# A projection stage without a loop, its low parts taken from PSUM, and the value bias added in attention

## The reference, cut to what matters

```python
qkv = x @ c_attn_w.T + c_attn_b
q, k, v = (heads(t) for t in jnp.split(qkv, 3, axis=2))      # 16 heads of 16
q_lat = q @ q2l_w.T + q2l_b                                  # 32 latents a head
k_lat = k @ kv2l_w.T + kv2l_b
v_lat = v @ kv2l_w.T + kv2l_b
q_lat = q_lat * cos + _rotate_half(q_lat) * sin
k_lat = k_lat * cos + _rotate_half(k_lat) * sin
q_for_k = q_lat @ wqk_w.T + wqk_b
att = jnp.einsum('bhql,bhkl->bhqk', q_for_k, k_lat) * L ** (-0.5)
y_lat = jnp.einsum('bhqk,bhkl->bhql', softmax(causal(att)), v_lat)
```

## Time and profile before

| | us |
|---|---|
| median of 3 runs (3117.6 to 3118.45) | 3118.36 |
| the profiled execution | 3112.8 |
| its span, first to last instruction | 3111.2 |
| busy PE / DVE / ACT / GpSimd | 2844.3 / 2273.6 / 1858.7 / 776.4 |
| projection, to attention's first load | 452.35 |
| attention, from there to its last y | 1794.3 |

### The profile page before, as it was taken

How to read it: one execution, slowest core, us unless ns; L and a number is a source line. 1 busy time by engine, 2 the same in 40 slices (tenths; PEclk the granted TensorE clock), 3 DMA queues, 4 the chain that set the end, 5 groups by cost and what they waited for, 6 DMA issues and landing times. The chain is left out here.

```text
span 3111.2 us, 50281 instructions
## 1 busy us (share of the span) xinstructions
PE 2844.3 (91%) x16538; PEld 1923.9 (62%) x16538; DVE 2273.6 (73%) x5659; ACT 1858.7 (60%) x3718; POOL 776.4 (25%) x701
## 2 busy tenths in 40 slices
PE   7888957999999999999999999999889997899990
PEld 5677744555555555555555555555367775799990
DVE  7999967888888888888888888888134543445443
ACT  4666632576667666666766676666535443546544
POOL 5777851010000001000110000010024444123220
PEclk9999986899999999999999999999989998899995
DMA  4666674242243234314332432340083220434316
GB/s 153 225 224 223 217 233 105 52 101 54 52 103 78 54 76 97 69 43 102 77 78 52 103 78 54 76 95 14 11 299 117 93 76 20 118 71 109 69 21 223
DMA packets 259647, 320.07 MB, mean 103 GB/s; under 512 B 70578, under 2 KB 157787, under 8 KB 258144
## 3 DMA queue, kind: packets, MB, share of 16 engines
q1 hardware_dynamic: 241760, 294.09, 33.4%
q0 software_dynamic: 17664, 23.19, 3.9%
HBM read 182.76 MB, written 143.95 MB: 105 GB/s over the span
## 5 line engine op out<-in xcount | busy, mean ns | idle before, releaser
L803 ACT ACTIVATE att_probs<-att_score_bank 128x512 f32<-128x512 f32 (+3 forms) x2560 | 1159.0, 551 | 608.5 <-PE att_score_bank L732 600.3
L840 DVE TENSOR_REDUCE att_partial_max<-att_max_bank 128x1 f32<-128x512 f32 x1536 | 1004.9, 687 | 124.3 <-PE att_max_bank L720 118.8
L720 PE MATMUL att_max_bank<-att_k_st,att_q_st 96*128 96x512 f32 (+3 forms) x2560 | 906.4, 389 | 31.8 <-DMA att_ident<-in_ident 20.9
L732 PE MATMUL att_score_bank<-att_q_st,att_k_st 98*128 98x512 f32 (+3 forms) x2560 | 924.5, 390 | 10.1 <-DMA att_q_st<-att_max_rows 7.6
L732 PEld LDWEIGHTS att_score_bank<-att_q_st,att_k_st 98*128 98x128 f32 x2560 | 481.8, 191 | 273.2 <-ACT att_probs L803 145.7
L720 PEld LDWEIGHTS att_max_bank<-att_k_st,att_q_st 96*128 96x128 f32 x2560 | 489.4, 193 | 244.7 <-DVE att_partial_max L840 100.7
L844 DVE CUSTOM_DVE_ANT_0 att_edge_sum<-att_max_bank,att_edge 128x128 f32<-128x128 f32 (+3 forms) x1024 | 482.0, 484 | 165.2 <-PE att_max_bank L720 164.7
L826 POOL TENSOR_SCALAR_AFFINE_SELECT att_probs<-att_probs 128x512 f32<-128x512 f32 x256 | 162.5, 635 | 1615.1 <-ACT att_probs L803 1615.1
L746 PE MATMUL att_acc_bank<-att_probs,att_v_st 128*32 128x512 f32 (+3 forms) x5120 | 544.2, 538 | 1.8 <-POOL att_probs L826 0.9
L210 POOL TENSOR_TENSOR proj_op_low<-proj_turned,proj_op_high 128x512 fp32r<-128x512 f32 x192 | 275.0, 1462 | 59.1 <-ACT proj_op_high L332 58.9
L746 PEld LDWEIGHTS att_acc_bank<-att_probs,att_v_st 128*32 128x32 f32 x5120 | 131.9, 109 | 245.2 <-issue 140.3
(11 more groups left out here) (221 smaller groups left out, 3887.3 us busy)
## 6 DMA issues: line engine op xcount, KB each, us to landing
qk_parts<-proj_parts SPq DMA_DIRECT2D x64, 1024.0 KB, 4.6
att_q_st<-qk_parts SPq DMA_DIRECT2D x192, 256.0 KB, 4.0
att_k_st<-qk_parts SPq DMA_DIRECT2D x192, 256.0 KB, 6.1
v_tokens<-proj_v_tok SPq DMA_DIRECT2D x64, 256.0 KB, 4.4
att_v_st<-v_tokens SPq DMA_DIRECT2D x64, 256.0 KB, 6.9
exp_w<-in_ew SPq DMA_DIRECT2D x16, 1024.0 KB, 8.9
dispatched<-mix_empty_rows SPq DMA_DIRECT2D x8, 1036.0 KB, 14.5
exp_rows<-dispatched SPq DMA_DIRECT2D x16, 518.0 KB, 5.5
```

Source lines behind the costliest of these rows:

```text
L720: nc.tensor.matmul(max_ps[u % MAXB][:, 0:width], q_st[0:3 * L, n % QBUF, j, t * P:(t + 1) * P], k_st[0:3 * L, g % 2, kb, j, 0:width], star ...
L732: nc.tensor.matmul(score_ps[h % SCOREB][:, q0:CH], k_st[:, g % 2, kt // TT, j, (kt % TT) * P:(kt % TT + 1) * P], q_st[:, n % QBUF, j, q0:C ...
L803: nc.scalar.activation(probs[:, k % PROBS, j, q0:CH], score_ps[(HG * k + j) % SCOREB][:, q0:CH], ACT.Exp).then_inc(exped, 1)
L840: nc.vector.tensor_reduce(best, bank[:], AX.X, ALU.max).then_inc(unit_reduced, 1)
```

## The change

project_heads is rewritten; attend is touched in four places.

- The loop is gone: all 64 units are written out, and every wait is on a constant.
- `q_full` and `k_full` are gone. DVE adds `k_cos` to `fin_k` in its PSUM bank (`add_k`), ACT rounds the high parts from the two banks (`high_q`, `high_k`), and DVE makes the low parts from the banks (`low_q`, `low_k`). The bank is free for PE when its low part is done. The factor SCALE is in the folded weight (`wqk_scaled`) instead of ACT's instruction.
- DVE's order in a unit: q's ropes, the low k of an earlier unit, k's ropes, `add_k`, `low_q`.
- `parts` has three buffers.
- The values are copied by ACT, two instructions a chunk (`copy_v`), without their bias, and stored one to two units later (`store_v`, ahead of the third unit's parts).
- PE waits for q's latents and k's latents apart (`roped`), so a latent bank of q can be written while k's ropes run.
- At the start the loads have semaphores of their own; ACT makes the high parts of the folded weights and DVE the low ones; wv is loaded last and split after the first ropes; GpSimd fills `v_tok`; wqk, the biases and the tables are waited for only where they are used.
- In attend, GpSimd adds b_v to `y` (`bias_y`, 64 times), and SyncE stores y after that. b_v is loaded there; edge is waited for by DVE alone, and ident and b_v by GpSimd and at the first `turn_sums`.

```diff
-    NU = NC * G
+    UNITS = B * NC * G
+    XCHUNKS = B * NC
     LAG = 2
     OPS = 4
+    PARTS = 3
...
-        q_full = sb("q_full", [P, 2, CH])
-        k_full = sb("k_full", [P, 2, CH])
-        parts = sb("parts", [P, 2, 4, CH], F32R)
+        parts = sb("parts", [P, PARTS, 4, CH], F32R)
...
+            load(0)
+            load(1)
+            nc.gpsimd.memset(v_tok[:, :, :, :, HD + 1:L], 0.0).then_inc(v_filled, 1)
+            nc.gpsimd.memset(v_tok[:, :, :, :, HD:HD + 1], 1.0).then_inc(v_filled, 1)
+            low_x(0)
...
+                if c % G == 1 and c // G + 1 < XCHUNKS:
+                    low_x(c // G + 1)
...
+            sp.dma_start(cq[:], a["c_attn_w"][0:C].rearrange("(g r) c -> r g c", r=64)).then_inc(q_fold_in, 16)
+            sp.dma_start(fold_q[:], a["fold_q"]).then_inc(q_fold_in, 16)
+            sp.dma_start(ck[:], a["c_attn_w"][C:2 * C].rearrange("(g r) c -> r g c", r=64)).then_inc(k_fold_in, 16)
+            sp.dma_start(fold_k[:], a["fold_k"]).then_inc(k_fold_in, 16)
+            for dst, src in ((wqk[:], a["wqk_t"]), (rot[:], a["rot"].rearrange("m p n -> p m n")), (b_cq[:], a["b_cq"]),
+                             (b_ck[:], a["b_ck"]), (b_small[:], a["b_small"])):
+                sp.dma_start(dst, src).then_inc(small_in, 16)
+            sp.dma_start(cos[:], a["cos"]).then_inc(tables_in, 16)
+            sp.dma_start(sin[:], a["sin"]).then_inc(tables_in, 16)
+            sp.dma_start(wv[:], a["wv_t"].rearrange("(k p) n -> p k n", p=P)).then_inc(wv_in, 16)
+
+            def store_v(n):
+                b, chunk = divmod(n, NC)
+                sp.wait_ge(v_filled, 2)
+                sp.wait_ge(v_copied, 2 * (n + 1))
+                for g in range(G):
+                    sp.dma_start(d["v"][b * G + g, chunk],
+                                 v_tok[:, n % 2, :, g * HG:(g + 1) * HG, :].rearrange("p t j l -> p t (j l)"),
+                                 ).then_inc(v_out[n % 2], 16)
+
+            for c in range(UNITS):
+                n, g = divmod(c, G)
+                b, chunk = divmod(n, NC)
+                if g == 2:
+                    store_v(n)
+                sp.wait_ge(q_split, c + 1)
+                sp.wait_ge(k_split, c + 1)
+                sp.dma_start(d["qk"][b * G + g, chunk].rearrange("f p n -> p f n"),
+                             parts[:, c % PARTS].bitcast(F32)).then_inc(parts_out[c % PARTS], 16)
...
+            pe.wait_ge(q_fold_in, 32)
+            fold(0, 0)
+            fold(0, 1)
+            pe.wait_ge(k_fold_in, 32)
+            fold(1, 0)
+            fold(1, 1)
+            pe.wait_ge(small_in, 5 * 16)
             nc.tensor.matmul(fin_q[:, 0:G], fold_q[:], b_cq[:], start=True, stop=True)
+            nc.tensor.matmul(fin_q[:, G:2 * G], fold_k[:], b_ck[:], start=True, stop=True).then_inc(folded, 1)
+            pe.wait_ge(weights_done, SCALED)
+            nc.tensor.matmul(fin_k[:, 0:P], rot[:, 0], wqk_scaled[:], start=True, stop=True).then_inc(folded, 1)
...
             def latents(c):
-                g, buf = c[1] % G, c[1] // G % 2
+                g, buf = c % G, c // G % 2
+                if c == 0:
+                    pe.wait_ge(weights_done, LAT_SPLIT)
                 if g == 0:
-                    pe.wait_ge(x_split, chunks(c, 1, 1))
-                if c[1] >= 2:
-                    pe.wait_ge(roped, units(c, 4, -4))
+                    pe.wait_ge(x_split, c // G + 1)
                 for x in range(2):
-                    product(lat[c[1] % 2][x][:], [
+                    if c >= 2:
+                        pe.wait_ge(roped, 4 * (c - 2) + 2 * x + 2)
+                    product(lat[c % 2][x][:], [
                         (w[:, k, g, :], xs[:, buf, k, :]) for k in range(KC) for w, xs in
                         ((lat_high[x], x_high), (lat_high[x], x_low), (lat_low[x], x_high))]).then_inc(lat_ready, 1)
 
             def finish(c):
 
-                high, low = op_high[:, c[1] % OPS], op_low[:, c[1] % OPS]
-                pe.wait_ge(lows_done, units(c, 3, 2))
-                pe.wait_ge(q_done, units(c, 1, FREE))
+                high, low = op_high[:, c % OPS], op_low[:, c % OPS]
+                if c == 0:
+                    pe.wait_ge(weights_done, WQK_SPLIT)
+                pe.wait_ge(lows_done, 3 * c + 2)
+                if c >= 1:
+                    pe.wait_ge(q_split, c)
                 product(fin_q[:], [(w[:, i, :], x[:, i]) for i in range(2) for w, x in
                                    ((wqk_high, high), (wqk_high, low), (wqk_low, high))]).then_inc(fin_q_ready, 1)
-                pe.wait_ge(lows_done, units(c, 3, 3))
-                pe.wait_ge(k_full_done, units(c, 1, FREE))
+                pe.wait_ge(lows_done, 3 * c + 3)
+                if c >= 1:
+                    pe.wait_ge(k_split, c)
                 product(fin_k[:], [(rot_r[:], high[:, 2]), (rot_r[:], low[:, 2])]).then_inc(fin_k_ready, 1)
...
+            def copy_v(n):
+                for pair in range(2):
+                    act.wait_ge(v_ready, 2 * n + pair + 1)
+                    if n >= 2:
+                        act.wait_ge(v_out[n % 2], 16 * G * (n // 2))
+                    nc.scalar.activation(v_tok[:, n % 2, 2 * pair:2 * pair + 2, :, 0:HD],
+                                         v_ps[pair][:].rearrange("p t (h e) -> p t h e", e=HD), ACT.Copy).then_inc(v_copied, 1)
+
+            def high_q(c):
+                act.wait_ge(fin_q_ready, c + 1)
+                if c == 0:
+                    act.wait_ge(weights_done, SCALED)
+                if c >= PARTS:
+                    act.wait_ge(parts_out[c % PARTS], 16 * (c // PARTS))
+                nc.scalar.activation(parts[:, c % PARTS, 0], fin_q[:], ACT.Identity, bias=b_qk[:]).then_inc(q_high_done, 1)
+
+            def high_k(c):
+                act.wait_ge(k_added, c + 1)
+                nc.scalar.activation(parts[:, c % PARTS, 2], fin_k[:], ACT.Copy).then_inc(k_high_done, 1)
+
+            high_x(0)
+            for x in range(2):
+                for k in range(KC):
+                    act.wait_ge(folded, KC * x + k + 1)
+                    nc.scalar.activation(flat(lat_high[x][:, k]), lat[x][k][:], ACT.Copy).then_inc(lat_high_done, 1)
+            for c in range(UNITS):
+                n, g = divmod(c, G)
+                if g == 0 and n:
+                    copy_v(n - 1)
+                high_op(c, 0)
+                high_op(c, 1)
+                if g == 1 and n + 1 < XCHUNKS:
+                    high_x(n + 1)
+                if c >= LAG:
+                    high_q(c - LAG)
+                high_op(c, 2)
+                if c >= LAG:
+                    high_k(c - LAG)
...
+            dve.wait_ge(small_in, 5 * 16)
+            nc.vector.tensor_scalar(wqk_scaled[:], wqk[:], SCALE, None, ALU.mult).then_inc(weights_done, 1)
+            for x in range(2):
+                for k in range(KC):
+                    dve.wait_ge(lat_high_done, KC * x + k + 1)
+                    nc.vector.tensor_tensor(flat(lat_low[x][:, k]), lat[x][k][:], flat(lat_high[x][:, k]).bitcast(F32),
+                                            ALU.subtract).then_inc(weights_done, 1)
+            dve.wait_ge(folded, BIASES_FOLDED)
...
+            dve.wait_ge(weights_done, BIASES_SET)
+            dve.wait_ge(tables_in, 32)
...
+            def add_k(c):
+                dve.wait_ge(fin_k_ready, c + 1)
+                nc.vector.tensor_tensor(fin_k[:], fin_k[:], k_cos[:, c % OPS], ALU.add).then_inc(k_added, 1)
+
+            def low_q(c):
+                dve.wait_ge(q_high_done, c + 1)
+                nc.vector.scalar_tensor_tensor(parts[:, c % PARTS, 1], fin_q[:], b_qk[:], parts[:, c % PARTS, 0].bitcast(F32),
+                                               ALU.add, ALU.subtract).then_inc(q_split, 1)
+
+            def low_k(c):
+                dve.wait_ge(k_high_done, c + 1)
+                nc.vector.tensor_tensor(parts[:, c % PARTS, 3], fin_k[:], parts[:, c % PARTS, 2].bitcast(F32),
+                                        ALU.subtract).then_inc(k_split, 1)
+
+            for c in range(UNITS):
+                rope(c, 0)
+                if c > LAG:
+                    low_k(c - LAG - 1)
+                rope(c, 1)
+                if c >= LAG:
+                    add_k(c - LAG)
+                    low_q(c - LAG)
+                if c == 0:
+                    dve.wait_ge(wv_in, 16)
+                    nc.vector.tensor_copy(wv_high[:], wv[:]).then_inc(weights_done, 1)
+                    dve.wait_ge(weights_done, WV_HIGH)
+                    nc.vector.tensor_tensor(wv_low[:], wv[:], wv_high[:].bitcast(F32), ALU.subtract).then_inc(weights_done, 1)
...
-                sp.wait_ge(y_done, n + 1)
+                sp.wait_ge(y_biased, n + 1)
                 sp.dma_start(d["y"][b, c, :, :, col:col + HG * HD],
                              y[:, n % 2].rearrange("p t j e -> p t (j e)")).then_inc(y_out[n % 2], 16)
 
             load(0)
```

(18 more changed lines are left out.)

312 lines of the change are left out of this document (108 added, 204 removed).

## The result

The changed kernel takes **3036.05 us** (3032.54 to 3037.71) where the kernel before took 3118.4 (3117.6 to 3118.84) on the same chip: a ratio of **0.9735**, 95% interval 0.9718 to 0.9752. The forecast was 3038. The profiled execution has a span of 3033.3 us, against 3111.2.

A forecast was written before the change was run, and what follows sets the result against it. The prediction took DVE to bound the projection, with PE next. Gains of 65 (body), 9.8 (start) and 7.1 (tail) less 1.2 (attention) make 80.7: 3118.4 - 80.7 = 3038 us, forecast 3030 to 3047, range 3027 to 3060.

The forecast's parts named there:

- What bounds before: Projection: DVE busy 370.70 of 370.70 us, 6.39 us a unit, its SBUF low parts held up by GpSimd's runs.
- Part 1, the prices: Projection: low parts reading PSUM cost 0.66 and 0.60 us, so DVE's unit falls from 6.39 to 4.50 us.
- The bound from above: Projection: low parts stay at 1.64 and 1.34 us if GpSimd's lock also held for PSUM operands.
- What is late next, and the body: Projection's body: PE binds at 5.26 us a unit; body goes from 393.0 to 328 us, gain 65 (59 to 68).
- Rival 1: Projection: hand-offs or a lower clock keep PE at 5.60 us a unit, gain 49, 3054 us; chance 0.16.
- Rival 2: Projection: the DMA engines bind at 236 GB/s, 5.97 us a unit, gain 26, 3077 us; chance 0.06.
- Part 2, the start: Start of projection: PE waits for cq and fold_q only, latents begin at 18.1; gain 9.8 us (7.5 to 11).
- Part 3, the tail: End of projection: 18.6 us shrink to 11.5, v stores already out; gain 7.1 us (6 to 8.5).
- Part 4, attention: Attention: load order +0.5 us, GpSimd's b_v additions 0.65 us each, last store 0.75 later; loss 1.2 (0 to 17).
- Rival 4: Attention: GpSimd's add delays masks and PE; slower above 1.3 us a chunk, 3198 us at 2.5; chance 0.02.
- The sum: Whole kernel: 65 + 9.8 + 7.1 - 1.2 = 80.7 us gained, 3118.4 to 3038 us.

The follow-up runs named there:

- run 3: Changed kernel with only k's low part taken from two SBUF tiles (k_cos added into k_full), GpSimd's work in full: 3112.36 us, ratio 0.998.
- run 4: Changed kernel with k's low part from two SBUF tiles and both GpSimd subtractions cut to 64 of 512 columns after the first units: 3037.98 us, 0.9749.
- run 1: Changed kernel with both low parts again taken from two SBUF tiles, ScalarE also writing q_full: 3105.82 us, ratio 0.9964.
- run 8: Kernel before with four buffers of parts in place of two, nothing else changed: 3114.77 us, ratio 0.9989.
- run 5: Changed kernel with both GpSimd subtractions cut to 64 of 512 columns after the first units: 3034.62 us, ratio 0.9727.
- run 2: Changed kernel with both low parts from SBUF and GpSimd's op_low cut to 64 of 512 columns from the fifth unit on: 3064.19 us, ratio 0.9826.
- run 6: Changed kernel with ScalarE writing q's full value a second time into an SBUF tile nothing reads: 3037.13 us, ratio 0.9742.
- run 7: Changed kernel with two buffers of parts in place of three: 3042.14 us, ratio 0.9758.
- run 9: Changed kernel with TensorE waiting for all loads of the start before it folds: 3047.18 us, ratio 0.9776.
- run 12: Changed kernel with attention's load of b_v issued behind the loads of all four chunks: 3038.91 us, ratio 0.975.
- run 10: Changed kernel with b_v added by VectorE in the projection again and nothing of it in attention: 3036.37 us, ratio 0.9743.
- run 11: Changed kernel without GpSimd's additions of b_v in attention, b_v still loaded: 3037.38 us, ratio 0.9746.

## Why the prediction was right, step by step

**What bounds before.** Right. That the price of a low part is GpSimd's hold on VectorE is shown in the changed kernel (runs 3 and 4); the kernel before was not run with GpSimd's work cut, but run 1, with its low parts, has its unit again. The 65.8 us of waits for stores were cheap (3 us, run 8).

**Part 1, the prices.** The prediction says that no row shows a subtraction from PSUM. The trace of the kernel before has one at its start, with GpSimd idle, and at the price that was taken:

```profile
24.07 0.68 DVE L361 TENSOR_TENSOR proj_q_lat_low<-proj_lat0q_bank,proj_q_lat_high 128x512 fp32r<-128x512 f32 x1
```

Low parts forecast at the rope's and the sum's rows; they measured 0.740 and 0.681, the sum in place in PSUM 0.687 (taken: 0.68). VectorE's unit comes to 255.05 / 56 = 4.55 us, forecast 4.50. The bound from above, the lock on PSUM operands too, is out (run 5). The Trainium skill, "VectorE: DVE Perf Modes", section "The TRN2 errata", has PSUM reads 65 ns dearer. Runs don't bear it out for this form: 0.683 us on two SBUF tiles where GpSimd keeps quiet (run 4) against 0.681 with one operand in PSUM. The rule that speaks for the edit, on another page of the Trainium skill, is weighed in the last section.

**What is late next, and the body.** Right in mechanism and size: 66.6 us against 65. PE never waits between 45 and 340 us, at clock 1.00, where I had allowed for some loss by taking 0.230 us a matmul. Rival 1 (5.60 us a unit by short waits) did not come, since there were none. Rival 2 did not either: 272 GB/s at a share of 0.78.

**Part 2, the start.** The step that was mis-sized: 12.8 us where I had 9.8, beyond my bound of 11. I put fold_q's landing at 9.8, from its 7.4 us in before. It landed at 7.07, 5.4 us after its issue, as the second load and not the third, with ck's 256 KB behind it and no longer ahead. That is 2.7 of the 3.0 us, in one profile: in the ten others that do not gate the folding it began between 6.0 and 7.5, and the latents between 15.4 and 16.4. The two other terms missed by less and against each other: from folding to the latents 8.9 us (8.3 forecast), from there to unit 0's finish 12.0 (12.9).

**Part 3, the tail.** 7.1 and 7.1, with the v stores out ahead of the last parts as foreseen.

**Part 4, attention.** Forecast a loss of 1.2; the two profiles show 5.2 to the last y and 3.4 behind it. An addition took 0.732 us, not 0.65. The 3.4 are scatter: behind the last y, the two profiles with the attention code of before (before and run 8) take 864.5 and 869.2 us. The 5.2 stay open. From the first load to the last y, the ten profiles with the additions (the changed kernel, runs 1 to 7, 9 and 12) take 1795.6 to 1803.2 us, 1799.8 on average, and the four without (before, runs 8, 10 and 11) 1794.3 to 1797.2, 1795.6 on average. So the profiles lean to a loss of some 4 us, while the medians of whole runs show none (run 11, without additions: 3037.38; run 12, with them, in the same session: 3038.91). A cost of a few us is neither shown nor ruled out. Rival 4, with its 1.3 us and more a chunk, is out.

**The sum.** 86.5 us gained in the projection, 8.6 given back behind it, in one pair of profiles: 77.9 against a forecast of 80.7; the medians differ by 82.3. The start came out 3 us better and the stretches behind the projection about 7 worse, which partly cancelled: that the total came within 2 us is in part luck, the body's gain is not.

## What to carry to other kernels

When a VectorE line with two SBUF inputs takes far longer than lines of its size that read PSUM, and GpSimd is busy beside it, leave one operand in PSUM: here the place of one operand of one instruction per unit decided over nearly the whole gain of 82 us. When you put a price on a stall, ask in which instructions it falls and which engine then stands behind them, for my sum said 5 to 25 us, the same sum with the measured price says 30, and 76 were paid. Buffers and moved work are worth what they free on the engine that binds: four buffers gave 3 us in before, for 65.8 us of waits, and values taken off VectorE gave nothing once PE was the limit.
